# A four-layer graph network on one core: how the second layer's normalised rows are formed

## The reference, cut to what matters

```
def _layernorm(x, axis=-1, eps=1e-05):
    m = mean(x); v = var(x)
    return (x - m) / sqrt(v + eps)

x = _layernorm(x + L0(x))    # relu((x + A x) W1 + b1) W2 + b2
x = _layernorm(x + L1(x))    # h = relu(x W1 + b1) W2 + b2;  h + A^T h
x = _layernorm(x + L2(x))    # see below
x = _layernorm(x + L3(x))    # edge messages relu(x[src] + edge_attr), two products, batch norm

L2:  h   = x * (deg_out ** -0.5)[:, None]
     agg = segment_sum(h[src], dst) * (deg_in ** -0.5)[:, None]
     return agg @ W + b
```

## Time and profile before

| | us |
|---|---|
| median of 3 runs | 590.97 (589.76 to 594.39) |
| the profiled execution, its own time | 594.86 |
| its span, first to last instruction | 593.2 |
| PE busy | 495.4 (84%) |
| DVE busy | 395.8 (67%) |
| POOL busy | 302.5 (51%) |
| ACT busy | 251.9 (42%) |

### The profile page before, as it was taken

How to read it: one execution, slowest core, us unless ns; L and a number is a source line. 1 busy time by engine, 2 the same in 40 slices (tenths; PEclk the granted TensorE clock), 3 DMA queues, 4 the chain that set the end, 5 groups by cost and what they waited for, 6 DMA issues and landing times.

```text
span 593.2 us, 7933 instructions
## 1 busy us (share of the span) xinstructions
PE 495.4 (84%) x2461; PEld 345.9 (58%) x2461; DVE 395.8 (67%) x894; ACT 251.9 (42%) x435; POOL 302.5 (51%) x328
## 2 busy tenths in 40 slices
PE   4999999999999998999992546578569876889875
PEld 2544459997899964899881101134235543465775
DVE  7999986768848959111672646565694776787375
ACT  7677751121285126410124424434435343444335
POOL 8999838301004005850004777777777777773000
PEclk9999999999999999999996567779979899899979
DMA  7900000000000400000947899999999999973004
GB/s 263 270 1 0 2 2 1 0 0 2 0 1 2 143 0 0 2 0 0 371 178 299 299 395 371 385 396 389 393 388 358 399 397 399 354 193 95 1 1 173
DMA packets 35604, 102.64 MB, mean 173 GB/s; under 512 B 6635, under 2 KB 7277, under 8 KB 35562
## 3 DMA queue, kind: packets, MB, share of 16 engines
q1 hardware_dynamic: 22150, 58.51, 26.4%
q0 software_dynamic: 13344, 43.53, 20.4%
q10 hardware_dynamic: 68, 0.09, 0.0%
HBM read 96.99 MB, written 5.12 MB: 172 GB/s over the span
## 4 chain that ended last, share of the span: by engine, by line
PE 42%; POOL 15%; DMA 14%; DVE 14%; issue 7%; ACT 5%; DVEq 3%; ACTq 0%; SPq 0%; POOLq 0%
DMA xg<-x_dram,srcT_i 13%; PE ps L1200 12%; POOL xg L490 11%; PE ps L1239 10%; PE ps L1212 7%; POOL hot_lo L426 4%; DVE ea L1020 3%; DVE hot_code L815 3%; PE ps L1268 2%; PE ps L1361 2%; PE ps L1382 2%; PE ps L1393 2%; ACT countsT L592 2%; DVEq L1028 2%; PE ps L1155 1%
## 5 line engine op out<-in xcount | busy, mean ns | idle before, releaser
L490 POOL DMA_INDIRECT xg<-x_dram,srcT_i x168 | 171.8, 1022 | 109.3 <-DMA x_dram<-xn 57.5
L1361 PE MATMUL ps<-ea,hot_w 128*32 128x512 f32 x336 | 94.5, 706 | 68.0 <-ACT ea L657 67.9
L1020 DVE TENSOR_TENSOR ea<-ea,xg 128x512 f32<-128x512 f32 x168 | 108.8, 689 | 35.1 <-DMA xg<-x_dram,srcT_i 34.7
L657 ACT ACTIVATE ea<-ea 128x2048 f32<-128x2048 f32 x41 | 78.3, 1910 | 110.3 <-DVE ea L1020 110.3
L1361 PEld LDWEIGHTS ps<-ea,hot_w 128*32 128x32 f32 x336 | 17.6, 120 | 123.5 <-ACT ea L657 72.9
L426 POOL TENSOR_SCALAR hot_lo<-iota_n,src_loT 128x128 bf16<-128x128 f16 x105 | 65.9, 644 | 4.8 <-PE ps L1155 3.9
L1035 DVE TENSOR_TENSOR x3T<-x3T,ps 128x128 f32 x84 | 24.3, 289 | 45.0 <-issue 26.0
L815 DVE TENSOR_SCALAR hot_code<-iota_c,codeT 128x380 bf16<-128x380 f16 x168 | 49.2, 352 | 2.4 <-issue 0.8
L1382 PEld LDWEIGHTS ps<-x3T,w_s 128*128 128x128 f32 x224 | 35.9, 200 | 9.6 <-issue 5.8
L1177 PE MATMUL ps<-w_s,xT 128*128 128x512 f32 (+1 forms) x80 | 41.1, 595 | 0.0
L1382 PE MATMUL ps<-x3T,w_s 128*128 128x180 f32 (+4 forms) x224 | 39.6, 332 | 1.1 <-ACT h L675 1.1
(11 more groups left out here) (180 smaller groups left out, 950.6 us busy)
## 6 DMA issues: line engine op xcount, KB each, us to landing
ea<-in_edge_attr_dram SPq DMA_DIRECT2D x41, 1024.0 KB, 9.7
w_s<-in_L_gnn_W_dram SPq DMA_DIRECT2D x5, 1024.0 KB, 8.8
xg<-x_dram,srcT_i POOLq DMA_INDIRECT x168, 7.4
xn<-in_x_dram SPq DMA_DIRECT2D x3, 768.0 KB, 8.4
x_dram<-xn SPq DMA_DIRECT2D x9, 256.0 KB
out_dram<-xn SPq DMA_DIRECT2D x9, 256.0 KB
w_s<-in_L_gnn_W_dram SPq DMA_DIRECT2D x2, 512.0 KB, 11.5
b_b<-in_L_gnn_b_dram SPq DMA_DIRECT2D x3, 256.0 KB, 10.0
```

What stands on the lines that cost most here:

```text
L490: pool.indirect_dma_start(out=xg[0:n, slot, r, :], out_offset=None, in_=x3_dram[:, :], in_offset=bass.IndirectOffsetOnAxis(ap=srcT_i[0:n, ...
L657: act.activation(ea[s][:, :, :], ea[s][:, :, :], ACT.Relu).then_inc(relu_done, 1)
L1020: dve.tensor_tensor(ea[s][0:n, r, :], ea[s][0:n, r, :], xg[0:n, slot, r, :], ALU.add).then_inc(add_done, 1)
L1361: ins = pe.matmul(ps[at_w:at_w + EW, 4 + g // 2 % 2, :], hot_w[:, g % RING, 2 * b + r, :], ea[g % RING][:, 2 * b + r, :], start=(r == 0), ...
```

## The change

VectorE no longer normalises layer 1's rows. It leaves the sums in `xn` and works out two numbers per row: `xs_s = rstd * deg^-0.5` and `xs_b = -mean * xs_s`. ScalarE forms `xs_hi` and `xs_f` from the un-normalised rows as `xs_s * xn + xs_b`, now with a scale and a bias per row, and `xs_hi` first. POOL normalises `xn` in place behind its low parts and the weight split, all ten tiles, and only then adds the bias `b2_b`. Mean, deviation and reciprocal of the ten tiles get buffers of their own (`mv3`, `std3`, `rstd3`, which the last norm uses too); three small memsets are added ahead of layer 0's norm.

```
+            pool.wait_ge(x1_coef, 1)
             for j in range(NT):
+                pool.tensor_scalar(xn[0:rows(j), j, :], xn[0:rows(j), j, :], rstd3[0:rows(j), j:j + 1], nmr3[0:rows(j), j:j + 1],
+                                   ALU.mult, ALU.add).then_inc(x_ready, 1)
+            for j in range(NT):
+                pool.wait_ge(x_ready, NT + j + 1)
                 pool.tensor_tensor(xn[0:rows(j), j, :], xn[0:rows(j), j, :], b2_b[0:rows(j), :], ALU.add).then_inc(xb_ready[2], 1)
...
             def scale_x(j):
-                act.wait_ge(x_ready, NT + j + 1)
+                r, one = slice(0, rows(j)), slice(j, j + 1)
+                act.wait_ge(xs_coef, 2 * j + 2)
                 if j >= 2:
                     act.wait_ge(xs_ready, j - 1)
-                if j == 0:
-                    act.wait_ge(deg_ready, 1)
-                act.activation(xs_f[0:rows(j), j % 2, :], xn[0:rows(j), j, :], ACT.Copy, scale=deg[0:rows(j), 1, j:j + 1])
-                act.activation(xs_hi[0:rows(j), j, :], xn[0:rows(j), j, :], ACT.Copy, scale=deg[0:rows(j), 1, j:j + 1]).then_inc(xs_done, 1)
+                act.activation(xs_hi[r, j, :], xn[r, j, :], ACT.Identity, bias=xs_b[r, one], scale=xs_s[r, one])
+                act.activation(xs_f[r, j % 2, :], xn[r, j, :], ACT.Identity, bias=xs_b[r, one], scale=xs_s[r, one]).then_inc(xs_done, 1)
...
+            dve.memset(std3[:, :], 1.0)
+            dve.memset(rstd3[:, :], 1.0)
+            dve.memset(mv3[:, :, :], 1.0)
...
-            layer_norm(1, lambda j: dve.wait_ge(xb_ready[1], j + 1), plus_x)
+
+            def scale_coefs(j):
+
+                n, r, one = NT + j, slice(0, rows(j)), slice(j, j + 1)
+                dve.wait_ge(std_ready, n + 1)
+                dve.reciprocal(rstd3[r, one], std3[r, one]).then_inc(rstd_ready, 1)
+                dve.wait_ge(rstd_ready, n + 1)
+                dve.tensor_scalar(xs_s[r, one], rstd3[r, one], deg[r, 1, one], None, ALU.mult).then_inc(xs_coef, 1)
+                dve.wait_ge(xs_coef, 2 * j + 1)
+                dve.tensor_scalar(xs_b[r, one], mv3[r, j, 0:1], xs_s[r, one], -1.0, ALU.mult, ALU.mult).then_inc(xs_coef, 1)
+
+            dve.wait_ge(deg_ready, 1)
+            for j in range(NT):
+                n, r = NT + j, slice(0, rows(j))
+                dve.wait_ge(xb_ready[1], j + 1)
+                dve.wait_ge(y_done, n + 1)
+                dve.tensor_tensor(xn[r, j, :], ps[r, 4 + n % 2, :], xn[r, j, :], ALU.add).then_inc(y_read, 1)
+                dve.wait_ge(y_read, n + 1)
+                dve.bn_stats(stats[r, n % 2, :], xn[r, j, :]).then_inc(ln_step, 1)
+                dve.wait_ge(ln_step, 2 * n + 1)
+                dve.bn_aggr(mv3[r, j, :], stats[r, n % 2, :]).then_inc(ln_step, 1)
+                if j:
+                    scale_coefs(j - 1)
+            scale_coefs(NT - 1)
+            dve.scalar_tensor_tensor(out=nmr3[:, :], in0=mv3[:, :, 0:1].rearrange("p j a -> p (j a)"), scalar=-1.0, in1=rstd3[:, :],
+                                     op0=ALU.mult, op1=ALU.mult).then_inc(x1_coef, 1)
```

More of the change, by code:

```diff
@@ L236, in gnn_kernel @@
         nmr3 = sb("nmr3", [P, NT], F32)
+        xs_s = sb("xs_s", [P, NT], F32)
+        xs_b = sb("xs_b", [P, NT], F32)
         deg = sb("deg", [P, 4, NT], F32)
@@ L275, in gnn_kernel @@
         xs_done, xs_ready = sem("xs_done"), sem("xs_ready")
+        xs_coef, x1_coef = sem("xs_coef"), sem("x1_coef")
         x3_stored = sem("x3_stored")
@@ L623, in scale_x @@
             def scale_x(j):
-                act.wait_ge(x_ready, NT + j + 1)
+                r, one = slice(0, rows(j)), slice(j, j + 1)
+                act.wait_ge(xs_coef, 2 * j + 2)
                 if j >= 2:
                     act.wait_ge(xs_ready, j - 1)
-                if j == 0:
-                    act.wait_ge(deg_ready, 1)
-                act.activation(xs_f[0:rows(j), j % 2, :], xn[0:rows(j), j, :], ACT.Copy, scale=deg[0:rows(j), 1, j:j + 1])
-                act.activation(xs_hi[0:rows(j), j, :], xn[0:rows(j), j, :], ACT.Copy, scale=deg[0:rows(j), 1, j:j + 1]).then_inc(xs_done, 1)
+                act.activation(xs_hi[r, j, :], xn[r, j, :], ACT.Identity, bias=xs_b[r, one], scale=xs_s[r, one])
+                act.activation(xs_f[r, j % 2, :], xn[r, j, :], ACT.Identity, bias=xs_b[r, one], scale=xs_s[r, one]).then_inc(xs_done, 1)
             for j in range(NT):
-                sqrt_var(NT + j)
+                act.wait_ge(ln_step, 2 * (NT + j) + 2)
+                act.activation(std3[0:rows(j), j:j + 1], mv3[0:rows(j), j, 1:2], ACT.Sqrt, bias=eps_s[0:rows(j), 0:1]).then_inc(std_ready, 1)
                 if j >= 2:
```

## The result

The changed kernel takes 590.34 us (median of 22 runs, 588.59 to 592.84), the kernel before 592.44 (22 runs, 589.76 to 595.30): a ratio of 0.9964, interval 0.9950 to 0.9979, which is 2.1 us less (1.2 to 3.0). That lies within 1%, and inside the forecast's range. The forecast of 588.6 is 1.7 low. Most of that, 1.5 us, is the base: the three runs that it started from have their median at 590.97, the 22 at 592.44. The gain itself was forecast as 2.4.

A forecast was written before the change was run, and what follows sets the result against it. VectorE's in-order list was taken as the bound, with a fixed tail behind it. Eight periods gaining 2.80 us less the tail's 0.42 gave 2.4, so 590.97 - 2.4 = 588.6 us, range 586.0 to 592.6.

The forecast's parts named there:

- The bound and the pass-through: VectorE's in-order list paces layer 1's norm, then a fixed tail; TensorE's later work gains whole whatever the stage gains.
- The period: VectorE's time from one tile's sum to the next: 1.97 us in place of 2.32, 2.80 gained over eight.
- The bound of 2.12: VectorE's longest expected period: each tiny instruction costs 0.16 plus 0.04 us for a wait, leaving a gain of 1.6.
- The tail: ScalarE and POOL's last tiles: pairs of copies 0.21 us longer, paid twice, 0.42 lost; TensorE resumes at 240.21.
- POOL's ten: POOL's ten normalisations behind the weight split: 0.64 to 2.58 us each, upper end taken, 25.8 in all, costing nothing.
- the cover: POOL's slack before layer 2's norm reads its bias sums: 9.7 us to spare, gone at 3.55 per normalisation.
- Rival B: VectorE's tiny instructions wait for POOL's low parts: period 2.42 us, 592.2 us in all; chance 0.11.
- Rival C: POOL's normalisations exceed 3.55 us each and layer 2's norm waits; at 4.0 each, 593.1 us; chance 0.04.
- Rival D: The stage's gain is real but lost behind it, in the transfer-filled last layer: 591.0 us; chance 0.13.
- TensorE's pace: TensorE's products in layer 1: six tiles in 10.85 us, 1.81 each, so it keeps ahead of VectorE.
- the bound of 4.1: Largest gain in VectorE's periods if the new work cost nothing and TensorE's 1.81 us per tile ruled: 8 x 0.51.

The follow-up runs named there:

- e1: The changed kernel with constants in place of the per-row operands of both tiny instructions; periods of 1.98 us, stage 25.34, single run 588.51 us.
- e3: The changed kernel with ScalarE's two copies scaled only, no bias (Copy in place of Identity); last sum to resumption 7.41 us, single run 591.23 us.
- e11: The changed kernel with three more POOL passes over the ten tiles before the bias sums; stage 26.15 us, single run 646.35 us on a slow chip.
- e8: The changed kernel with six more POOL passes before the bias sums; a loss of 8.7 us at the first gather, single run 649.52 us on a slow chip.
- e2: The changed kernel with both tiny instructions in forms with two tensors as inputs; periods of 2.32 us, stage 28.01, single run 590.42 us.
- e12: The changed kernel with its tiny instructions spread between wide ones; 587.59 us, ratio 0.9904 to the kernel before; stage 23.21 us.
- e5: First run of the same spread-order kernel as e12, on a slow chip; ratio 0.976 to the kernel before, stage 23.21 us.
- e7: The changed kernel with VectorE, not POOL, normalising the ten tiles behind its last coefficients; stage 26.44 us, single run 652.92 us on a slow chip.

## Why the prediction was right, and where it was off

**The bound and the pass-through** held. VectorE's list set the period up to the last tile, the rest was a fixed tail, and what the stage gained appeared unchanged 75 us later.

**The period** is the term that was mis-sized. I had it at 1.72 + 0.17 + 0.08 = 1.97, and it measured 2.09; so eight periods gave 1.84 and not 2.80. The 1.72 held. The two prices behind it came from the earlier trace rows, whose instructions have immediates or two tensors as inputs, while the new ones take a value per row. e1 gives the forecast's period when that operand is gone. The bound of 2.12 held it, by adding 0.04 for each instruction, a guess for the right kind of cost. The rows to go by were there in kind: ScalarE's, where the earlier trace rows show what a per-row operand adds. I used that on ScalarE and forgot it on VectorE. That the timed difference, 2.1 us, came out near the forecast's 2.4 is no support for the size: the stage gave 1.48, and the interval of 1.2 to 3.0 cannot tell the two.

**The tail** was forecast at +0.42 and measured +0.39, and e3 shows the second per-row operand, the bias, as its cause (with the change of function not separated). The resumption came at 240.16, against 240.21 forecast. That this is so near is partly luck, since the execution was 1.0 us early ahead of the stage, which made up for the period.

**POOL's ten** took 0.75 each, near the lower end of 0.64 to 2.58. I had chosen the upper end as the one that can hurt. It changed nothing, for the cover is long: e11 shows 17.85 us more on POOL hidden whole, and e8 where it ends.

**Rival B** is refuted for the change, and shown for its neighbour in e2. I gave it 0.11 because the row against it had one partition and no per-row operand. The instruction with 128 partitions and such an operand behaved like that row: a tensor_scalar of one element does not wait, a tensor_tensor of one element does. **Rival C** was off by a factor of nearly five in what POOL would have had to take. **Rival D**, the gain lost further on, has nothing for it in the traces up to the first gather. Behind it the stretch to the end differs by some 4 us between kernels (271.4 to 275.6), in which a loss of 1.5 could not be seen; that it is not lost rests on the times, and best on e12, where the interval of 4.0 to 7.4 holds the stage's 4.44.

**TensorE's pace** was misread, to no effect on the forecast. I divided 10.85 us by six tiles. That counts the last product's run-out and, more, a wait for VectorE: the sixth tile's bank came free with the sum that ran from 221.02 to 221.70, and its first weight load starts at 221.82. 24 products 0.43 apart and a run-out of 0.16 make 10.46, so the wait is 0.39 of the 10.85. Without one a tile takes 1.716, as e12's products show. It entered the bound of 4.1, which would have been 4.8 less the tail's 0.42, and e5's expectation of 1.81.

## What to carry to other kernels

Price a tiny instruction from a row with the same kind of operand: a value per row added 0.06 us to one of 0.15, and as much to what waits for it. Where its result is not wanted at once, put it behind a wide instruction that it does not depend on; there it was free, while two of them in a row, the second waiting for the first, cost 0.38 us per tile. Moving work to an idle engine can be worth more than its own time when the two engines make each other wait: 0.15 of the 0.23 us per tile was such waiting. And look at the next stage too: in e7 the work that VectorE kept for later cost 0.27 us in the changed stage and 4.3 in all.

## What the runs showed of the hardware that was not expected

- A VectorE tensor_tensor on one element per row took 1.02 us where it began 1.00 before the end of POOL's low part, and 0.16 alone or in the last 0.14 of one; a tensor_scalar on one element with a per-row operand took 0.21 beside one and alone.
- On VectorE a per-row operand makes a one-element tensor_scalar 0.21 us long in place of 0.15. On POOL a tensor_scalar on 512 elements takes 0.75 with two such operands and 0.59 with immediates.
- VectorE's tensor_scalar on 512 elements took 0.54 us in POOL's pauses, 1.48 to 1.64 beside its low parts and bias sums, and 4.83 beside a weight split of 4.70 that had begun just before it (e7). In the kernel before, three that began within the last 0.3 us of a low part lost at most 0.02, and four that began earlier in it took 0.92 to 0.94.
- After 6.2 us without work TensorE ran four products in 2.04 us in place of 1.09, at a granted clock of 0.50 (e8).
